# A transformer layer on eight cores: the down projection's two passes cut at 256 instead of 512 tokens, the second over all eight PSUM banks

## The chip, the cores and the metric

One Trainium2 chip, all 8 cores, one program on each with its own slice of the work and no exchange between cores. The time is device microseconds of the slowest core.

## The reference

Layer norm, then attention with ALiBi bias, then a feed-forward branch with Walsh-Hadamard transforms, whose gate multiplies the attention's output (batch 2, 4096 tokens, E = 2048, 16 heads, inner width I = 8192):

```python
xn = layernorm(x)
s = attention(xn)                                  # causal, ALiBi, 16 heads
h = fwht(xn * SU_ug) / 64
u = silu(h @ W_gate.T * sc_gate) * (h @ W_up.T * sc_up)
z = fwht(u * SU_dp) / 64                           # over I = 8192
f = z @ W_down.T * (Wscale_dp * 64)
out = x + s * silu(f)
```

## The kernel before

Each core takes one batch's keys and values and a quarter of its queries: TOKF = 1024 tokens. Everything is held transposed, features on partitions and tokens on columns. A small scheduler (`Sched`) keeps one list of operations per engine. An engine runs its list strictly in the order in which `OP` was called for it, and an operation begins with waits on semaphores (L108 and L125 are the helper's waits). Nothing is reordered.

The program runs in phases: K and V projections (L491, L530), Q (L621), attention (L730 to L773), the output projection (L816), whose result s goes to `s_dram`; then the feed-forward branch. There the up and gate projections (L912) fill `U`, a tile of 64 row blocks (I / 128) of 1024 tokens in SBUF. The transform over I is done in two parts: within 128 rows by a matmul with a Hadamard matrix (L952, evicted by ACT at L958), and over the 64 row blocks by VectorE, in 32 slices of 32 tokens. A slice reads U (L976, L977), makes four rounds in `C1`/`C2` (L996, L998), and its last round writes U back (L1005, L1008).

The down projection, the part in question, follows in two passes over tokens, pass 0 with tokens 0 to 511 and pass 1 with the rest (`FHT` = 512). Each pass has four groups `eog` of 512 output features, that is four blocks `e4` of 128, each of which accumulates in a PSUM bank of its own (`pb`, eight banks of 512 fp32 columns). A group is 16 steps. For each step POOL loads four row blocks x 512 features of `wdT` (L1036, fp32 in memory, bf16 in SBUF, 512 KB there) into one of five ring slots `wdring`, and PE makes 16 matmuls 128x128 by 128x512 (L1048). A load waits for the matmuls of five steps before. Groups alternate between banks 0 to 3 and 4 to 7, so a group's first matmul waits for the evictions of the group before the last. It waits for the transform too: pass 0 for slice 16 (`ev_zH`), pass 1 for slice 32 (`ev_z`).

A finished bank goes through four steps. ACT evicts it with SiLU into `g_st` (L1070), and issues the loads of s (`ss_st`, L1077) and x (`xf_st`, L1083) from its own queue. VectorE combines them (`tensor_mul` into `o_st`, L1089; `tensor_add` into `res_st`, L1093). SP stores the result (L1103). All of these buffers have two halves (`par`), so an eviction waits for the combine of two before (`prev2`). A combine also waits for the store of the one before (`prev_out`):

```python
prev2 = ev_comb.get(gc - 2)
prev_out = ev_outs[gc - 1] if gc >= 2 else None
```

Since the combines are put on VectorE's list after the loop over slices, none can run before slice 32 is done.

Of the kernel before, what the change touches and what calls it, by code (L numbers as in the profile page):

```python
# [9 lines left out]
AF = mybir.ActivationFunctionType  # L10
# [122 lines left out]
def build_program(cfg):  # L133
    S, E, I, QG = cfg.S, cfg.E, cfg.I, cfg.QG
    FT, IT, H = cfg.FT, cfg.IT, cfg.H
    NSLOT, CS = cfg.NSLOT, cfg.CS
    TOKF = cfg.TOKF
# [3 lines left out]
    FH = TOKF // 2  # L141
# [7 lines left out]
    NSL = TOKF // CS  # L149
# [9 lines left out]
    xfT_d = din("xfT", [E, TOKF])  # L159
# [18 lines left out]
    out_d = nc.dram_tensor("out", [E, TOKF], F32, kind="ExternalOutput").ap()  # L178
# [115 lines left out]
    def Uap(it, c0, w):  # L294
        t = Us[it // ITQ]
        base = (it % ITQ) * TOKF
        return t[:, base + c0: base + c0 + w]
# [663 lines left out]
    ev_h2_last = ev_h2_ev[(IT - 1, UPC - 1)]  # L961

    ev_z = None
    ev_zH = None
    for sl in range(NSL):
        sl0 = sl * CS
        ename = "vector"
        cA, cB = C1, C2

        def p4_sA(eng, sl0=sl0, cA=cA):  # L970
            q = ITQ
            for half, (ua, ub) in enumerate(((Us[0], Us[2]), (Us[1], Us[3]))):
                a = ua.rearrange("p (t c) -> p t c", c=TOKF)[:, :, sl0:sl0 + CS]
                b = ub.rearrange("p (t c) -> p t c", c=TOKF)[:, :, sl0:sl0 + CS]
                c3 = cA.rearrange("p (t c) -> p t c", c=CS)
                eng.tensor_add(c3[:, half * q:(half + 1) * q, :], a, b)  # L976
                ins = eng.tensor_sub(  # L977
                    c3[:, 2 * q + half * q:2 * q + (half + 1) * q, :], a, b)
            return ins
        ev_sA = OP(ename, p4_sA,  # L980
                   waits=[ev_h2_last if sl == 0 else ev_z,
                          ev_ug_mm[(IT - 1, 1)] if sl == 0 else None])

        ev_stg = ev_sA
        src, dst = cA, cB
        for st in range(nst2 - 2, -1, -1):
            d = 1 << st
            last = (st == 0)

            def p4_s2(eng, src=src, dst=dst, d=d, last=last, sl0=sl0):  # L990
                if not last:
                    s4 = src.rearrange("p (g two w) -> p g two w", two=2,
                                       w=d * CS)
                    d4 = dst.rearrange("p (g two w) -> p g two w", two=2,
                                       w=d * CS)
                    eng.tensor_add(d4[:, :, 0, :], s4[:, :, 0, :],  # L996
                                   s4[:, :, 1, :])
                    return eng.tensor_sub(d4[:, :, 1, :], s4[:, :, 0, :],  # L998
                                          s4[:, :, 1, :])
                s4 = src.rearrange("p (g two w) -> p g two w", two=2, w=CS)  # L1000
                for uq in range(4):
                    utv = Us[uq].rearrange("p (t two c) -> p t two c", two=2,
                                           c=TOKF)[:, :, :, sl0:sl0 + CS]
                    gg = uq * (ITQ // 2)
                    eng.tensor_add(utv[:, :, 0, :],  # L1005
                                   s4[:, gg:gg + ITQ // 2, 0, :],
                                   s4[:, gg:gg + ITQ // 2, 1, :])
                    ins = eng.tensor_sub(utv[:, :, 1, :],  # L1008
                                         s4[:, gg:gg + ITQ // 2, 0, :],
                                         s4[:, gg:gg + ITQ // 2, 1, :])  # L1010
                return ins
            ev_stg = OP(ename, p4_s2, waits=[ev_stg])
            src, dst = dst, src
        ev_z = ev_stg
        if sl == NSL // 2 - 1:
            ev_zH = ev_z

    ev_wd_ld = {}
    ev_dn_mm = {}
    ev_gs = {}  # L1020
    ev_comb = {}
    ev_outs = []
    gld = 0
    gc = 0
    NEOG = FT // 4
    FHT = FH
    for ps in range(2):
        tk0 = ps * FHT
        ev_zg = ev_zH if ps == 0 else ev_z
        for eog in range(NEOG):  # L1030
            g2 = ps * NEOG + eog
            for it4 in range(IT // K2):
                slot = gld % NWDR
                prev_mm = ev_dn_mm.get(gld - NWDR)
                ev_wd_ld[(ps, eog, it4)] = OP("gpsimd",
                    (lambda eng, eog=eog, it4=it4, slot=slot: eng.dma_start(  # L1036
                        wdring[slot].rearrange("p (b c) -> p b c", b=K2),
                        wdT_d[it4 * K2 * 128:(it4 + 1) * K2 * 128,
                              eog * 512:eog * 512 + 512].rearrange(
                                  "(b p) c -> p b c", p=128))),  # L1040
                    waits=[ev_u_all, prev_mm], dma="wd%d" % slot)

                def p4_dn(eng, eog=eog, it4=it4, slot=slot, tk0=tk0, g2=g2):
                    bk0 = (g2 % 2) * 4
                    for iti in range(K2):
                        it = it4 * K2 + iti
                        for e4 in range(4):
                            ins = eng.matmul(  # L1048
                                pb[bk0 + e4][:, 0:FHT],
                                wdring[slot][:, iti * 512 + e4 * 128:  # L1050
                                             iti * 512 + e4 * 128 + 128],
                                Uap(it, tk0, FHT),
                                start=(it == 0), stop=(it == IT - 1))
                    return ins
                ws = [ev_wd_ld[(ps, eog, it4)]]
                if it4 == 0:
                    ws += [ev_zg]
                    ws += [ev_gs.get((g2 - 2, kkk)) for kkk in range(4)]
                ev_dn_mm[gld] = OP("tensor", p4_dn, waits=ws)
                gld += 1  # L1060

            for e4 in range(4):
                eo = eog * 4 + e4
                par = gc % 2
                bk = (g2 % 2) * 4 + e4
                prev2 = ev_comb.get(gc - 2)
                prev_out = ev_outs[gc - 1] if gc >= 2 else None

                ev_g = OP("scalar", (lambda eng, bk=bk, eo=eo, par=par:
                    eng.activation(g_st[:, par * FHT:(par + 1) * FHT],  # L1070
                                   pb[bk][:, 0:FHT], AF.Silu,
                                   scale=dnvec[:, eo:eo + 1])),
                    waits=[ev_dn_mm[gld - 1], prev2])
                ev_gs[(g2, e4)] = ev_g

                ev_ss = OP("scalar", (lambda eng, eo=eo, tk0=tk0, par=par:
                    eng.dma_start(ss_st[:, par * FHT:(par + 1) * FHT],  # L1077
                                  s_dram[eo * 128:(eo + 1) * 128,
                                         tk0:tk0 + FHT])),
                    waits=ev_sd_all + [prev2, ev_zg], dma="st%d" % par)  # L1080

                ev_xf = OP("scalar", (lambda eng, eo=eo, tk0=tk0, par=par:
                    eng.dma_start(xf_st[:, par * FHT:(par + 1) * FHT],  # L1083
                                  xfT_d[eo * 128:(eo + 1) * 128,
                                        tk0:tk0 + FHT])),
                    waits=[prev2, ev_zg], dma="st%d" % par)

                def p4_comb(eng, par=par):
                    sch.chain("vector", eng, eng.tensor_mul(  # L1089
                        o_st[:, par * FHT:(par + 1) * FHT],  # L1090
                        g_st[:, par * FHT:(par + 1) * FHT],
                        ss_st[:, par * FHT:(par + 1) * FHT]))
                    return eng.tensor_add(  # L1093
                        res_st[:, par * FHT:(par + 1) * FHT],
                        o_st[:, par * FHT:(par + 1) * FHT],
                        xf_st[:, par * FHT:(par + 1) * FHT])
                ev_cb = OP("vector", p4_comb,
                           waits=[ev_g, ev_ss, ev_xf, prev_out])
                ev_comb[gc] = ev_cb

                ev_outs.append(OP("sync", (lambda eng, eo=eo, tk0=tk0,
                                           par=par:
                    eng.dma_start(out_d[eo * 128:(eo + 1) * 128,  # L1103
                                        tk0:tk0 + FHT],
                                  res_st[:, par * FHT:(par + 1) * FHT])),
                    waits=[ev_cb], dma="outd"))
                gc += 1

    n_out = sch.cnt["outd"]
    sch.ops["sync"].append(  # L1110
# [87 lines left out]
```

How the kernel before makes its waits and increments, by code:

```python
    def chain(self, eng_name, E, ins):  # L103
        s = self.sem(self.esem[eng_name] + "ch")
        self.cnt[self.esem[eng_name] + "ch"] += 1
        v = self.cnt[self.esem[eng_name] + "ch"]
        ins.then_inc(self.sems[self.esem[eng_name] + "ch"], 1)
        E.wait_ge(self.sems[self.esem[eng_name] + "ch"], v)
# [7 lines left out]
            def body(E, lst=lst):  # L116
                done = {}
                for fn, ws, ev in lst:
                    need = {}
                    for (s, v, _b) in ws:
                        if v > need.get(s, 0):
                            need[s] = v
                    for s, v in need.items():
                        if v > done.get(s, 0):
                            E.wait_ge(self.sems[s], v)
                            done[s] = v
                    ins = fn(E)
                    if ev is not None:
                        ins.then_inc(self.sems[ev[0]], ev[2])
# [268 lines left out]
        def p1_stats(eng, par=par, ev_s=ev_sq[slab]):  # L398
            for ft in range(FT):
                eng.matmul(pb[0][0:1, 0:128], ones128_b[:],
                           xTb[par][:, ft * 128:ft * 128 + 128],
                           start=(ft == 0), stop=(ft == FT - 1))
            eng.wait_ge(sch.sems[ev_s[0]], ev_s[1])
            for ft in range(FT):
                ins = eng.matmul(pb[0][0:1, 128:256], ones128_b[:],
                                 sq_scr[:, ft * 128:ft * 128 + 128],
                                 start=(ft == 0), stop=(ft == FT - 1))
            return ins
```

## Time and profile before

| | us |
|---|---|
| median of 2 runs | 4943.36 (4925.18 to 4961.55) |
| profiled execution | 4600.18 |
| its span, core 7 | 4598.6 |
| spans of the eight cores | 4572.6 to 4598.6 |
| PE busy in the span | 3423.3 (74%) |
| DVE busy | 1863.6 (41%) |
| ACT busy | 956.5 (21%) |

The profile is that of one execution, which took less than the timed ones; its span is the time from the first to the last instruction of the slowest core. Times within it are microseconds from the span's start. The granted clock is the share of TensorE's full 2.4 GHz.

### The profile page before, as it was taken

To read this page: it belongs to the slowest core of one execution; us is meant where nothing else is said; L and a number is where in the kernel's file an instruction comes from. 1 tells how busy PE (TensorE), PEld (TensorE's weight loads), DVE (VectorE), ACT (ScalarE), POOL (GpSimd) and SP (SyncE) were. 2 spreads that over 40 slices of the span, in tenths; PEclk is the share of its full clock that TensorE was granted. 3 is DMA by queue.
4 is the path that set the end of the run, shared out by engine and by line. 5 is a ranking of instruction groups with operands and counts; after the bars stand their busy time and mean duration, and the time that the engine had idled before them with its cause. 6 is when DMAs were issued, how large, how long until landed. Compare 5 with 4: busy or idle time off the path is not lost.

```text
span 4598.6 us, 61740 instructions; the slowest of 8 cores (4572.6 to 4598.6 us)
## 1 busy us (share of the span) xinstructions
PE 3423.3 (74%) x22715; PEld 1784.6 (39%) x22715; DVE 1863.6 (41%) x3576; ACT 956.5 (21%) x2347; POOL 293.5 (6%) x309
## 2 busy tenths in 40 slices
PE   0499796997995677788884929999999910634887
PEld 0276575765762222222221804444444300211333
DVE  0244444444440166667773060000000079995001
ACT  0121121211211234444442211111111420000000
POOL 0000000000000000000000001111111100100111
PEclk9899898998997777778776959999999965867999
DMA  9323232232324221111104118888889600645999
GB/s 147 28 44 52 42 53 42 43 55 39 51 42 74 61 56 37 46 28 37 37 19 74 40 12 78 76 76 77 75 73 77 66 0 0 89 65 89 177 172 155
DMA packets 633739, 287.94 MB, mean 63 GB/s; under 512 B 520675, under 2 KB 614883, under 8 KB 631267
## 3 DMA queue, kind: packets, MB, share of 16 engines
q0 software_dynamic: 422880, 191.55, 37.5%
q1 hardware_dynamic: 107652, 42.10, 4.2%
q10 hardware_dynamic: 102912, 50.35, 4.2%
q8 instruction: 187, 3.06, 0.3%
q14 instruction: 108, 0.88, 0.1%
HBM read 429.34 MB, written 46.14 MB: 103 GB/s over the span
## 4 chain that ended last, share of the span: by engine, by line
PE 64%; DVE 20%; DMA 6%; issue 3%; SPq 3%; another core or an unknown queue 2%; ACT 1%; DVEq 0%; ACTq 0%; POOLq 0%
PE pb L912 18%; PE pb L530 9%; PE pb L491 9%; PE pb L751 5%; PE pb L734 5%; PE pb L1048 4%; PE pb L730 4%; DMA wdring<-wdT 4%; DVE C L996 3%; DVE C L998 3%; SPq L307 3%; PE pb L816 2%; PE pb L621 2%; DVE rinv L667 2%
## 5 line engine op out<-in xcount | busy, mean ns | idle before, releaser
L912 PE MATMUL pb<-xnTf,wring 128*128 128x512 bf16 x4096 | 889.2, 380 | 5.2 <-DMA wring<-wupT 3.9
L1048 PE MATMUL pb<-U,wdring 128*128 128x512 bf16 x2048 | 457.4, 385 | 419.8 <-DVE U L1008 247.3
L763 DVE SCALAR_TENSOR_TENSOR pb<-mwin_s,slopes_l,pb 128x256 f32<-128x256 f16 x1019 | 484.0, 482 | 471.4 <-PE pb L751 451.4
L912 PEld LDWEIGHTS pb<-xnTf,wring 128*128 128x128 bf16 x4096 | 401.4, 98 | 492.9 <-issue 14.0
L773 ACT ACTIVATE ET<-pb 128x256 bf16<-128x256 f32 x1019 | 390.0, 384 | 486.2 <-DVE pb L763 393.8
L491 PE MATMUL pb<-xnT,wk_b 128*128 128x128 bf16 x8192 | 485.2, 222 | 0.0
L491 PEld LDWEIGHTS pb<-xnT,wk_b 128*128 128x128 bf16 x8192 | 471.5, 99 | 10.9 <-issue 1.0
L530 PE MATMUL pb<-wv_b,xnT 128*128 128x512 bf16 x2048 | 454.8, 383 | 16.9 <-DVE vstg L543 16.9
L1048 PEld LDWEIGHTS pb<-U,wdring 128*128 128x128 bf16 x2048 | 200.1, 99 | 676.9 <-issue 449.4
L936 DVE TENSOR_TENSOR U<-A_st,B_st 128x1024 bf16<-128x1024 f32 x64 | 78.4, 1225 | 830.0 <-ACT B_st L928 830.0
L730 PE MATMUL pb<-ET,vh 128*128 128x256 bf16 x1019 | 331.7, 326 | 9.5 <-DMA vh<-v_scr 4.0
L751 PE MATMUL pb<-q_sb,kh 128*128 128x256 bf16 x1019 | 307.1, 323 | 25.2 <-DMA kh<-k_scr 25.2
L734 PE MATMUL pb<-ET,ones_b 128*1 128x256 bf16 x1019 | 311.3, 305 | 0.0
L530 PEld LDWEIGHTS pb<-wv_b,xnT 128*128 128x128 bf16 x2048 | 200.5, 99 | 257.1 <-issue 28.1
L506 ACT ACTIVATE kstg<-pb,bk_l 128x128 bf16<-128x128 f32 x512 | 188.0, 367 | 243.4 <-PE pb L491 243.1
L543 DVE TENSOR_TENSOR vstg<-pb,bvB 128x512 bf16<-128x512 f32 x128 | 88.1, 691 | 352.0 <-PE pb L530 313.1
L466 DVE TENSOR_TENSOR xn_scr<-xTb,rstdB 128x128 f32<-128x128 bf16 x640 | 186.8, 292 | 76.3 <-ACT mrstdB L459 8.3
L1070 ACT ACTIVATE g_st<-pb,dnvec 128x512 bf16<-128x512 f32 x32 | 22.0, 687 | 863.7 <-PE pb L1048 546.7
L734 PEld LDWEIGHTS pb<-ET,ones_b 128*1 128x1 bf16 x1019 | 80.5, 79 | 268.3 <-issue 247.6
L674 PE MATMUL pb<-rinv,ones_f 1*128 1x256 f32 x128 | 63.3, 587 | 161.9 <-DVE rinv L667 161.9
L471 DVE TENSOR_TENSOR xnT<-xn_scr,mrstdB 128x128 bf16<-128x128 f32 x512 | 149.5, 292 | 54.1 <-DVE xn_scr L466 1.5
L751 PEld LDWEIGHTS pb<-q_sb,kh 128*128 128x128 bf16 x1019 | 95.9, 99 | 192.8 <-issue 129.9
(85 smaller groups left out, 2446.1 us busy)
## 6 DMA issues: line engine op xcount, KB each, us to landing
wdring<-wdT POOLq DMA_DIRECT2D x128, 512.0 KB, 12.6
wring<-wupT POOLq DMA_DIRECT2D x64, 512.0 KB, 9.5
wring<-wgT POOLq DMA_DIRECT2D x64, 512.0 KB, 9.0
xTb<-xT POOLq DMA_DIRECT2D x32, 512.0 KB, 8.7
k_scr<-kstg ACTq DMA_DIRECT2D x32, 512.0 KB, 5.0
v_scr<-vstg ACTq DMA_DIRECT2D x128, 128.0 KB, 1.9
kh<-k_scr SPq DMA_DIRECT2D x16, 1024.0 KB, 5.4
vh<-v_scr SPq DMA_DIRECT2D x16, 1024.0 KB, 9.5
```

The lines of the kernel that those rows point to most:

```text
L466: sch.chain("vector", eng, eng.tensor_mul(xn_scr[:], xTb[par][:, ft * 128:ft * 128 + 128], rstdB[:, par * 128:par * 128 + 128]))
L471: ins = eng.tensor_sub(dst, xn_scr[:], mrstdB[:, par * 128:par * 128 + 128])
L491: ins = eng.matmul(bank[:, 0:128], wk_b[:, (ft * H + hch) * 128:(ft * H + hch) * 128 + 128], xnT2[par2][:, ft * 128:ft * 128 + 128], start ...
L506: return eng.activation(kstg[par][:, hch * 128:hch * 128 + 128], bank[:, 0:128], AF.Identity, bias=bk_l[:, hch:hch + 1])
L530: ins = eng.matmul(bank[:, 0:512], xnT2[par2][:, ft * 128:ft * 128 + 128], wv_b[:, ft * E + vch * 512:ft * E + vch * 512 + 512], start=(ft ...
L730: eng.matmul(pvb[:, 0:QG], vh[hp][:, rho * 128:rho * 128 + 128], ETs[e4][:], start=(idx == 0), stop=(idx == W - 1))
L734: return eng.matmul(pb[6 + par][0:1, 0:QG], ones128_b[:], ETs[e4][:], start=(idx == 0), stop=(idx == W - 1))
L751: return eng.matmul(pb[b4][:, 0:QG], kh[hp][:, rho * 128:rho * 128 + 128], q_ap, start=True, stop=True)
L763: eng.scalar_tensor_tensor(pb[b4][:, 0:QG], mwin_s[:, coff:coff + QG], slopes_l[:, h:h + 1], pb[b4][:, 0:QG], ALU.mult, ALU.add)),
L773: eng.activation(ETs[e4][:], pb[b4][:, 0:QG], AF.Exp)),
L912: ins = eng.matmul(pb[bk0 + u][:, 0:UCH], wring[slot][:, ft * 128:ft * 128 + 128], xnTf[:, ft * TOKF + u * UCH:ft * TOKF + u * UCH + UCH], ...
L1048: ins = eng.matmul(pb[bk0 + e4][:, 0:FHT], wdring[slot][:, iti * 512 + e4 * 128: iti * 512 + e4 * 128 + 128], Uap(it, tk0, FHT), start=(it ...
```

## The change

The passes are no longer equal. Pass 0 takes tokens 0 to 255 in one chunk; pass 1 takes tokens 256 to 1023 in two chunks of 384. The gate of a pass is now worked out from its last token: slice 8 for pass 0, slice 32 for pass 1. In pass 0 a group still uses four banks, in turn. In pass 1 a group has two chunks x four feature blocks and uses all eight banks, so each step makes 32 matmuls of 384 columns from one load of the ring. The number of ring loads stays 128 (2 passes x 4 groups x 16), the columns multiplied stay the same, the matmuls grow from 2048 to 3072 (1024 of 256 columns and 2048 of 384), and evictions, combines and stores from 32 to 48 (16 of 256 columns, 32 of 384). The waits for banks are kept by bank (`bank_owner`) instead of by group.

```diff
-        if sl == NSL // 2 - 1:
-            ev_zH = ev_z
+        ev_z_at[sl] = ev_z
...
-    FHT = FH
-    for ps in range(2):
-        tk0 = ps * FHT
-        ev_zg = ev_zH if ps == 0 else ev_z
+    q4 = TOKF // 4
+    passes = [(0, [q4]), (q4, [3 * TOKF // 8, 3 * TOKF // 8])]
+    for ps, (tk0, chunks) in enumerate(passes):
+        gate_sl = (tk0 + sum(chunks) + CS - 1) // CS - 1
+        ev_zg = ev_z_at[gate_sl]
+        nck = len(chunks)
         for eog in range(NEOG):
             g2 = ps * NEOG + eog
+            if nck == 1:
+                bks = [(g2 % 2) * 4 + e4 for e4 in range(4)]
+            else:
+                bks = list(range(8))
...
                     for iti in range(K2):
                         it = it4 * K2 + iti
-                        for e4 in range(4):
-                            ins = eng.matmul(
-                                pb[bk0 + e4][:, 0:FHT],
...
-                                Uap(it, tk0, FHT),
-                                start=(it == 0), stop=(it == IT - 1))
+                        off = 0
+                        for ci, cw in enumerate(chunks):
+                            for e4 in range(4):
+                                ins = eng.matmul(
+                                    pb[bks[ci * 4 + e4] if len(chunks) > 1
+                                       else bks[e4]][:, 0:cw],
...
+                                    Uap(it, tk0 + off, cw),
+                                    start=(it == 0), stop=(it == IT - 1))
+                            off += cw
...
                 if it4 == 0:
                     ws += [ev_zg]
-                    ws += [ev_gs.get((g2 - 2, kkk)) for kkk in range(4)]
+                    ws += [bank_owner.get(b) for b in bks]
...
-            for e4 in range(4):
-                eo = eog * 4 + e4
-                par = gc % 2
-                bk = (g2 % 2) * 4 + e4
+            off = 0
+            for ci, cw in enumerate(chunks):
+                for e4 in range(4):
+                    eo = eog * 4 + e4
+                    bk = bks[ci * 4 + e4] if nck > 1 else bks[e4]
+                    par = gc % 2
+                    c0 = tk0 + off
...
+                    bank_owner[bk] = ev_g
```

The eviction, the two loads, the combine and the store are the same but for their width `cw` and their place `c0`.

PE's queue where the last group of pass 0 goes over to the first of pass 1, before:

```order
5189 L1048 MATMUL pb<-U_96,wdring_119 128x512 [waits s_wd3]
5190 L1048 MATMUL pb<-U_96,wdring_119 128x512 x15
5191 L1048 MATMUL pb<-U_93,wdring_120 128x512 [waits s_wd4,s_dve,s_act]
5192 L1048 MATMUL pb<-U_93,wdring_120 128x512 x15
5193 L1048 MATMUL pb<-U_93,wdring_116 128x512 [waits s_wd0]
```

The same place of the changed kernel (`U_93` to `U_96` are the four parts of U, `wdring_116` to `_120` the five slots; `s_act` stands for the banks):

```order
5189 L1056 MATMUL pb<-U_96,wdring_119 128x256 [waits s_wd3]
5190 L1056 MATMUL pb<-U_96,wdring_119 128x256 x15
5191 L1056 MATMUL pb<-U_93,wdring_120 128x384 [waits s_wd4,s_dve,s_act]
5192 L1056 MATMUL pb<-U_93,wdring_120 128x384 x31
5193 L1056 MATMUL pb<-U_93,wdring_116 128x384 [waits s_wd0]
```

One load of a slot now serves 32 matmuls of pass 1, and the wait on `s_act` is for the last of eight evictions instead of the last of four of the group before the last.

ACT's queue at the beginning of the down projection, before:

```order
1935 L1070 ACTIVATE g_st<-pb,dnvec 128x512 [waits s_pe]
1936 L1077 DMA ss_st<-s_scr 128x512 [waits s_dve]
1937 L1083 DMA xf_st<-xfT 128x512
1938 L1070 ACTIVATE g_st<-pb,dnvec 128x512
1939 L1077 DMA ss_st<-s_scr 128x512
1940 L1083 DMA xf_st<-xfT 128x512
1941 L1070 ACTIVATE g_st<-pb,dnvec 128x512 [waits s_dve]
```

And in the changed kernel:

```order
1935 L1084 ACTIVATE g_st<-pb,dnvec 128x256 [waits s_pe]
1936 L1093 DMA ss_st<-s_scr 128x256 [waits s_dve]
1937 L1100 DMA xf_st<-xfT 128x256
1938 L1084 ACTIVATE g_st<-pb,dnvec 128x256
1939 L1093 DMA ss_st<-s_scr 128x256
1940 L1100 DMA xf_st<-xfT 128x256
1941 L1084 ACTIVATE g_st<-pb,dnvec 128x256 [waits s_dve]
```

Only the widths moved: the third eviction waits for VectorE's first combine in both.

## Rows read from the trace of the kernel before

**Rows 1.** The cores' spans, slowest and fastest, with mean granted clock
```profile
core 4: 4572.6 us, clock 0.870
...
core 7: 4598.6 us, clock 0.866
```
**Rows 2.** The page's 40 slices of the span, in tenths busy, PE and DVE
```profile
PE   0499796997995677788884929999999910634887
...
DVE  0244444444440166667773060000000079995001
```
**Rows 3.** Timeline of PE from 3700 on: start, duration, count, idle before and releaser
```profile
3949.30 112.34 PE L1048 MATMUL pb<-U,wdring 128*128 128x512 bf16 x512 [247.29 <-DVE U L1008]
4198.54 29.43 PE L1048 MATMUL pb<-U,wdring 128*128 128x512 bf16 x128 [136.90 <-ACT g_st L1070]
4228.69 7.07 PE L1048 MATMUL pb<-U,wdring 128*128 128x512 bf16 x32 [0.72 <-DMA wdring<-wdT]
...
4491.07 34.69 PE L1048 MATMUL pb<-U,wdring 128*128 128x512 bf16 x160 [0.23 <-DMA wdring<-wdT]
...
4546.31 32.93 PE L1048 MATMUL pb<-U,wdring 128*128 128x512 bf16 x144 [2.34 <-DMA wdring<-wdT]
```
**Rows 4.** Timeline of DVE where the last slice ends
```profile
4194.40 0.42 DVE L1008 TENSOR_TENSOR U<-C 128x256 bf16<-128x256 f32 x1
4194.74 0.68 DVE L1089 TENSOR_TENSOR o_st<-g_st,ss_st 128x512 f32<-128x512 bf16 x1
```
**Rows 5.** Windows of core 7: busy time of PE, PEld, DVE, ACT, POOL; clock; DMA share; GB/s
```profile
3949.00:4062.00 113.00, 112.34 (x512) 50.45 (x512) 108.32 (x148) 1.38 (x2) 22.97 (x31) 0.98 1.04 144
4062.00:4198.00 136.00, 0.00 (x0) 0.00 (x0) 129.75 (x178) 0.98 (x2) 0.74 (x1) 0.51 0.07 12
4198.00:4390.00 192.00, 175.40 (x785) 76.28 (x786) 19.38 (x28) 10.02 (x15) 35.55 (x48) 0.98 1.10 175
4390.00:4580.00 190.00, 169.69 (x753) 73.39 (x751) 16.62 (x24) 7.48 (x11) 31.85 (x43) 0.97 1.05 166
4580.00:4599.00 19.00, 0.00 (x0) 0.00 (x0) 5.54 (x8) 2.15 (x4) 0.00 (x0) 0.61 0.43 138
```
**Rows 6.** Groups of the page: busy us, mean ns of one, idle before
```profile
L912 PE MATMUL pb<-xnTf,wring 128*128 128x512 bf16 x4096 | 889.2, 380 | 5.2 <-DMA wring<-wupT 3.9
L1048 PE MATMUL pb<-U,wdring 128*128 128x512 bf16 x2048 | 457.4, 385 | 419.8 <-DVE U L1008 247.3
```
**Rows 7.** Waits from 3700 on: us in total, times, longest
```profile
PE pb L1048 <- DMA wdring<-wdT: 35.5, 28, 4.0
```
**Rows 8.** Short matmuls in a free stream, and their weight loads by group
```profile
268.82 12.78 PE L491 MATMUL pb<-xnT,wk_b 128*128 128x128 bf16 x224
...
L491 PEld LDWEIGHTS pb<-xnT,wk_b 128*128 128x128 bf16 x8192 | 471.5, 99 | 10.9 <-issue 1.0
```
**Rows 9.** DMA issues: count, KB each, median us to landing
```profile
wq_b<-wqT POOLq DMA_DIRECT2D x1, 8192.0 KB, 53.1
```
**Rows 10.** Timeline of DVE and ACT after the last matmul
```profile
4579.39 0.69 ACT L1070 ACTIVATE g_st<-pb,dnvec 128x512 bf16<-128x512 f32 x1 [42.01 <-PE pb L1048]
...
4582.70 0.69 DVE L1089 TENSOR_TENSOR o_st<-g_st,ss_st 128x512 f32<-128x512 bf16 x1 [29.38 <-DMA xf_st<-xfT]
...
4586.86 0.69 DVE L1089 TENSOR_TENSOR o_st<-g_st,ss_st 128x512 f32<-128x512 bf16 x1 [2.67 <-DMA out<-res_st]
...
4594.70 0.69 DVE L1089 TENSOR_TENSOR o_st<-g_st,ss_st 128x512 f32<-128x512 bf16 x1 [2.20 <-DMA out<-res_st]
```
**Rows 11.** The same after the group that ends at 4323.7: eviction, then the combines
```profile
4323.81 0.69 ACT L1070 ACTIVATE g_st<-pb,dnvec 128x512 bf16<-128x512 f32 x1 [42.74 <-PE pb L1048]
...
4333.17 0.69 DVE L1089 TENSOR_TENSOR o_st<-g_st,ss_st 128x512 f32<-128x512 bf16 x1 [34.72 <-DMA xf_st<-xfT]
...
4343.12 0.69 DVE L1089 TENSOR_TENSOR o_st<-g_st,ss_st 128x512 f32<-128x512 bf16 x1 [8.46 <-DMA out<-res_st]
...
4352.58 0.69 DVE L1089 TENSOR_TENSOR o_st<-g_st,ss_st 128x512 f32<-128x512 bf16 x1 [7.98 <-DMA out<-res_st]
...
4360.80 0.69 DVE L1089 TENSOR_TENSOR o_st<-g_st,ss_st 128x512 f32<-128x512 bf16 x1 [6.73 <-DMA out<-res_st]
```
**Rows 12.** The chain of waits at the end: start, us, what
```profile
4579.26 0.02 issue
...
4584.26 2.50 DMA out<-res_st
...
4588.42 2.50 DMA out<-res_st
```

More of the change, by code:

```diff
@@ L963, in build_program @@
     ev_z = None
-    ev_zH = None
+    ev_z_at = {}
     for sl in range(NSL):
@@ L1022, in build_program @@
     ev_outs = []
+    bank_owner = {}
     gld = 0
@@ L1041, in build_program, with p4_dn @@
                     waits=[ev_u_all, prev_mm], dma="wd%d" % slot)
-                def p4_dn(eng, eog=eog, it4=it4, slot=slot, tk0=tk0, g2=g2):
-                    bk0 = (g2 % 2) * 4
+                def p4_dn(eng, eog=eog, it4=it4, slot=slot, tk0=tk0,
+                          chunks=chunks, bks=bks):
                     for iti in range(K2):
                         it = it4 * K2 + iti
-                        for e4 in range(4):
-                            ins = eng.matmul(
-                                pb[bk0 + e4][:, 0:FHT],
-                                wdring[slot][:, iti * 512 + e4 * 128:
-                                             iti * 512 + e4 * 128 + 128],
-                                Uap(it, tk0, FHT),
-                                start=(it == 0), stop=(it == IT - 1))
+                        off = 0
[4 more added lines that the diff above has]
+                                       else bks[e4]][:, 0:cw],
+                                    wdring[slot][:, iti * 512 + e4 * 128:
+                                                 iti * 512 + e4 * 128 + 128],
+                                    Uap(it, tk0 + off, cw),
+                                    start=(it == 0), stop=(it == IT - 1))
+                            off += cw
                     return ins
@@ L1057, in build_program @@
                     ws += [ev_zg]
-                    ws += [ev_gs.get((g2 - 2, kkk)) for kkk in range(4)]
+                    ws += [bank_owner.get(b) for b in bks]
                 ev_dn_mm[gld] = OP("tensor", p4_dn, waits=ws)
                 gld += 1
-            for e4 in range(4):
-                eo = eog * 4 + e4
-                par = gc % 2
-                bk = (g2 % 2) * 4 + e4
[L1066 to L1107, printed above, removed]
@@ new lines, in build_program, with p4_comb @@
+            off = 0
[5 more added lines that the diff above has]
+                    c0 = tk0 + off
+                    prev2 = ev_comb.get(gc - 2)
+                    prev_out = ev_outs[gc - 1] if gc >= 2 else None
+                    ev_g = OP("scalar", (lambda eng, bk=bk, eo=eo, par=par,
+                                         cw=cw:
+                        eng.activation(g_st[:, par * FH:par * FH + cw],
+                                       pb[bk][:, 0:cw], AF.Silu,
+                                       scale=dnvec[:, eo:eo + 1])),
+                        waits=[ev_dn_mm[gld - 1], prev2])
+                    ev_gs[(g2, ci * 4 + e4)] = ev_g
+                    bank_owner[bk] = ev_g
+                    ev_ss = OP("scalar", (lambda eng, eo=eo, c0=c0, par=par,
+                                          cw=cw:
+                        eng.dma_start(ss_st[:, par * FH:par * FH + cw],
+                                      s_dram[eo * 128:(eo + 1) * 128,
+                                             c0:c0 + cw])),
+                        waits=ev_sd_all + [prev2, ev_zg], dma="st%d" % par)
+                    ev_xf = OP("scalar", (lambda eng, eo=eo, c0=c0, par=par,
+                                          cw=cw:
+                        eng.dma_start(xf_st[:, par * FH:par * FH + cw],
+                                      xfT_d[eo * 128:(eo + 1) * 128,
+                                            c0:c0 + cw])),
+                        waits=[prev2, ev_zg], dma="st%d" % par)
+                    def p4_comb(eng, par=par, cw=cw):
+                        sch.chain("vector", eng, eng.tensor_mul(
+                            o_st[:, par * FH:par * FH + cw],
+                            g_st[:, par * FH:par * FH + cw],
+                            ss_st[:, par * FH:par * FH + cw]))
+                        return eng.tensor_add(
+                            res_st[:, par * FH:par * FH + cw],
+                            o_st[:, par * FH:par * FH + cw],
+                            xf_st[:, par * FH:par * FH + cw])
+                    ev_cb = OP("vector", p4_comb,
+                               waits=[ev_g, ev_ss, ev_xf, prev_out])
+                    ev_comb[gc] = ev_cb
+                    ev_outs.append(OP("sync", (lambda eng, eo=eo, c0=c0,
+                                               par=par, cw=cw:
+                        eng.dma_start(out_d[eo * 128:(eo + 1) * 128,
+                                            c0:c0 + cw],
+                                      res_st[:, par * FH:par * FH + cw])),
+                        waits=[ev_cb], dma="outd"))
+                    gc += 1
+                off += cw
```

## The prediction, made before the changed kernel ran

> **What bounds the kernel now.** I read from the outside in: the cores, the page's slices, and then only the end of the program, since nothing ahead of the last phase is changed. The eight cores end within 0.6% of each other [rows 1], so one core stands for all. The time line of the slices [rows 2] shows two PE holes near the end, where DVE works alone: that is the transform over 64 row blocks (32 slices of 32 tokens), of which the down projection is the reader.
>
> The PE timeline [rows 3] gives the program's last 900 us. PE is idle for 247.29 us until the 16th slice is done, then runs 512 matmuls of 512 columns in 112.34 us without one wait on data, is idle again for 136.90 us, and from 4198.54 runs the other 1536 until 4546.31 + 32.93 = 4579.24. The second hole is the important one. Its releaser is the eviction g_st on ACT, and the DVE rows [rows 4] say why that eviction was late: the combines (L1089, L1093) stand behind all 32 slices in DVE's queue. The slices' last piece is at 4194.40, and the first combine starts at 4194.74. Since the third eviction waits for the first combine, no third group of banks could be had before. So of pass 0's four groups only two ran under the transform: 512 of 2048 matmuls, a quarter of the columns. The last slice's end, about 4195, does not depend on PE, so it stays where it is. All that the change is worth is then decided in the stretch after it: 4198.5 to 4598.6 = 400.1 us.
>
> What limits that stretch? PE is busy in 89 to 91% of it [rows 5] with matmuls that cost 457.4/2048 = 0.223 us by their group and 34.69/160 = 0.217 when they run freely [rows 3, 6]. PE waits 35.5 us in 28 pieces for the weight ring [rows 7]. The DMA share stands at 1.05 to 1.10 in it [rows 5]. 1536 matmuls are 96 loads of the ring in 380.7 us, 3.97 us each, against 16 x 0.217 = 3.47 of matmul. So weights and PE are nearly balanced, and weights win slightly while combines share the DMA engines.
>
> **The change part by part.**
>
> Pass widths. Pass 0 is cut from 512 tokens to 256 with an earlier gate (slice 8 of 32), pass 1 grows to 768. But the queue order on DVE is the same, so again only groups 0 and 1 of pass 0 can run before the slices end. They need 32 loads; at 3.97 us each that is 127 us. A slice takes (4194.7 - 3949.3)/16 = 15.3 us [rows 3, 4], so the new gate, eight slices ahead of the old one, opens at about 3826, and the two groups are done by 3955, long before 4195. Cost: nothing, and the cover has 240 us to spare; and the earlier gate earns nothing, since this hole was never short. What was hidden before was 512 x 512 columns; now it is 512 x 256. Half of the hidden work comes out into the open: 131,072 columns, about 55 us of PE at 0.217 per 512 if PE sets the pace.
>
> Rest of pass 0 (groups 2 and 3, 512 matmuls of 256 columns). Between the 128-column row (12.78/224 = 0.057 us) and the 512-column one (0.217) a straight line gives 0.110 for 256 columns and 0.164 for 384 [rows 3, 8]. Even the 128-column ones stream faster than their weight loads' 98 ns rows, so short matmuls have no floor that matters here. PE would need 512 x 0.110 = 57 us, 1.8 per ring load. The weights can't follow: five loads lie ready, 27 must come. Bounds for a load: 53.1/16 = 3.32 us, the large wq_b load cut into pieces of 512 KB [rows 9], and 3.97 with full combines beside it. Combines of half size run here, so I take 3.7: 27 x 3.7 = 100, with the first and last loads' matmuls 104. (57 if the ring could be fed at PE's pace; 111 at the high end.) In this part the change makes the starved side worse.
>
> From pass 0 to pass 1. The first matmul of each pass-1 group now waits for all eight banks, where it used to wait for four banks given up one group earlier. Behind that wait stand the group's 512 matmuls, and behind those ACT's evictions and POOL's ring loads, which find no free slot. To free the last bank of pass 0, ACT must evict number 15, which waits for combine 13. At the program's end [rows 10] PE's last matmul ends at 4579.26, the first combine starts at 4582.70, and the next ones follow about 4.15 us apart, since each waits for the output DMA of the one before (2.50 us in the chain [rows 12]). That is with idle DMAs. With the ring filling, the first came 9.4 us after its eviction and the periods were 9.95, 9.46 and 8.22 [rows 11]. Idle: 3.4 + 3.8 + 1.8 = 9; loaded: 9.4 + 9.2 + 1.8 = 20. I take 15.
>
> Pass 1. 4 x 512 matmuls of 384 columns: 2048 x 0.164 = 335 us. Each ring load now serves 32 matmuls = 5.2 us, above 3.97, so the 35.5 us of waits for weights go; PE sets the pace. That is the gain, and it is small.
>
> Three drains between groups of pass 1. PE stops at the last matmul, and the eighth eviction waits for the sixth combine: 3.4 to the first, 5 periods, a combine of 1.2, an eviction of 0.6. A period at 384 columns: 4.15 less a quarter each of two 0.69 us VectorE pieces, with the output DMA left at 2.50, is 3.8. So 24 us, and 2 more for ring loads still in flight: 26 each, 78 in all. Bounds: 21 if the DMA shrinks with its bytes, 57 if the loaded periods of [rows 11] hold. I choose near the idle end because PE takes 5.2 us over a load, so one or two are in flight when it stops, not five. Before, these drains lay under the other four banks' matmuls.
> [...]
>
> Restarts. After the idle 136.90 us the first 128 matmuls took 29.43 instead of 27.8 [rows 3]; in the idle hole the granted clock is 0.51, the lower level of 1.2 GHz, and 0.97 to 0.98, nearly always 2.4 GHz, where PE works [rows 5]. Five starts x 1.6 = 8 us.
>
> Tail. Eight combines follow the last matmul instead of four: 3.4 + 7 x 3.8 + 3.5 = 33 us, where it was 19.3.
>
> Sum after 4198.5: 104 + 15 + 335 + 78 + 8 + 33 = 573 us, against 400.1: 173 more. The profiled execution took 4600.18 us (its span of 4598.6 and 1.6 around it), so it would become 4773, a ratio of 1.0376. The runs shown have a median of 4943.36, 7.5% above the profiled one, which the trace does not explain. I carry the ratio: 5129 (adding 173 gives 5116).
>
> **The rivals.**
>
> A, drains under load: the ring and the combines' own loads keep DMA full, and each drain costs 57, the first boundary 20. For it speak the 9.2 us periods in all of the stretch while the ring works; against it that the ring is full and silent some 15 us after PE stops. 573 + 93 + 5 = 671: 4871, ratio 1.059, 5235.
>
> B, weights arrive faster than I think: rest of pass 0 at PE's pace (57) and a boundary of 9. For it speaks that with the DMA share at 1.04 PE did not wait once for weights [rows 5, 3], so 3.5 us is no proven floor; against it the 28 waits after 4198. 573 - 47 - 6 = 520: 4720, ratio 1.026, 5072.
>
> C, not slower: all of pass 0 runs under the transform. With half the width, its 64 loads need 254 us, and from 3826 there are 370. Then 104 + 15 + 2 fall away: 452, 52 us more than now, 4652, ratio 1.011, 4999. It decides at combine 0: only if combines get onto DVE before the last slice. Against it stand DVE's rows [rows 4] and an order of the queue that the change leaves alone. Even then the drains must vanish too for a gain.
>
> D, shorter matmuls in a free stream. If the 0.217 us are a pace set by weights rather than by the array, halving the ring's traffic in pass 1 speeds matmuls up: at an assumed 0.114 us for 384 columns pass 1 takes 233, 471 in all, 4671, ratio 1.015, 5020. The gate's projections at 0.217 (889.2/4096 [rows 6]), with 5.2 us of idle in all, speak against it. The source of that 0.114 is the Trainium skill (TensorE: Matmul & The Clock Gate, "Back-to-back issue gap"), which gives about 131 ns for 512 columns and 81 for 128 in a stream of load and matmul pairs, and a line between them gives 114; this trace has 217 and 57 and disagrees at both ends.
>
> **How the numbers follow.** Forecast 0.75, A 0.10, B 0.10, C 0.03, D 0.01, and 0.01 for what I don't see. The forecast's own bounds: low 94 + 9 + 335 + 63 + 8 + 30 = 539 (5092), high 111 + 20 + 337 + 120 + 8 + 35 = 631 (5191). Reaching to B, and for the step from profile to median, the range is 5060 to 5200; A, C and D fall out, 0.14. Within 2% (about what a measurement of this kernel can tell from no change) lie C and D: 0.04. No case gives over 2% faster: 0.01 for the unseen. Slower by over 2%: 0.95.
>
> **What would show it.** PE idle from 3955 or so to 4195 though pass 0 began near 3826; 512 matmuls of 256 columns in about 104 us after it with many waits on wdring; three waits of PE on g_st of 24 to 30 us, at equal distances of about 110 us, with six combines in each; no wait on wdring in pass 1; eight outputs after the last matmul. I am wrong if a third group of pass 0 starts before 4190, if PE's waits at the boundaries of pass 1 are under 15 or over 40 us, or if a 384-column matmul costs other than 0.16 to 0.17 us.

## The result and the profile after

The changed kernel is slower: the ratio to the kernel before is 1.0384, 95% interval 1.0362 to 1.0405. The forecast had a ratio of 1.0376, but named 5129 us with a range of 5060 to 5200; the median of 11 runs is 4986.68 and falls outside it.

These two fit together only so: in some executions of either kernel the four cores of one die, or of both, show a lower granted clock (a mean down to 0.77 instead of 0.85 to 0.86 in the changed kernel), the two runs behind the 4943.36 of before are as slow as those, and without them before takes 4589 to 4615 us and the changed kernel 4771 to 4778 (4800.6 in its profiled execution), which are the times that are compared from here on.

Core 7 of the changed kernel can be laid beside core 7 of before. Cores of the changed kernel:

```profile
core 0: 4799.0 us, clock 0.853
...
core 7: 4771.0 us, clock 0.859
```

4771.0 - 4598.6 = 172.4 us more; the sum had 173. From PE's third group to the end it is 4771.0 - 4194.6 = 576.4 us instead of 400.1, that is 176.3 more; core 7 came to that group 3.9 us earlier than in the profile of before. (Core 0 is later still because its last slice ends 20 us later than that of core 7, at 4212.7, through phases that the change doesn't touch.)

The PE timeline of core 7, in the columns of [rows 3]:

```profile
3823.60 10.52 PE L1056 MATMUL pb<-U,wdring 128*128 128x256 bf16 x80 [124.29 <-DVE U L1008]
3834.32 1.91 PE L1056 MATMUL pb<-U,wdring 128*128 128x256 bf16 x16 [0.21 <-DMA wdring<-wdT]
...
4194.62 12.77 PE L1056 MATMUL pb<-U,wdring 128*128 128x256 bf16 x96 [269.30 <-ACT g_st L1084]
4211.15 1.91 PE L1056 MATMUL pb<-U,wdring 128*128 128x256 bf16 x16 [3.76 <-DMA wdring<-wdT]
...
4303.76 2.41 PE L1056 MATMUL pb<-U,wdring 128*128 128x256 bf16 x16 [0.29 <-DMA wdring<-wdT]
4321.41 85.26 PE L1056 MATMUL pb<-U,wdring 128*128 128x384 bf16 x512 [15.23 <-ACT g_st L1084]
4431.54 84.82 PE L1056 MATMUL pb<-U,wdring 128*128 128x384 bf16 x512 [24.87 <-ACT g_st L1084]
4542.20 85.79 PE L1056 MATMUL pb<-U,wdring 128*128 128x384 bf16 x512 [25.85 <-ACT g_st L1084]
4652.60 85.22 PE L1056 MATMUL pb<-U,wdring 128*128 128x384 bf16 x512 [24.60 <-ACT g_st L1084]
```

The whole story stands in these lines. Pass 0 starts 126 us earlier than before and then stands still for 269.30 us: the hole has grown, not gone. What starts at 4194.62 runs freely for six steps (96 matmuls) and then goes in steps of 16 matmuls, most of them 1.9 us long and with a wait for weights behind them, until 4306.2. Then come four blocks of 512 matmuls without one wait on the ring, each behind a wait for an eviction.

The DVE timeline where the last slice ends answers to [rows 4]:

```profile
4191.69 0.42 DVE L1008 TENSOR_TENSOR U<-C 128x256 bf16<-128x256 f32 x1
4192.02 0.41 DVE L1106 TENSOR_TENSOR o_st<-g_st,ss_st 128x256 f32<-128x256 bf16 x1
```

The first combine still comes straight behind the last slice, and PE's third group 2.6 us after it.

Waits of core 7 from 3700 on, as in [rows 7]:

```profile
PE pb L1056 <- ACT g_st L1084: 359.9, 5, 269.3
...
PE pb L1056 <- DMA wdring<-wdT: 83.0, 51, 4.3
```

Five waits for evictions instead of one. The waits for weights have more than doubled from 35.5 us, and all are in pass 0; but of the 83.0 us only 43.3 come after the last slice, where they cost time. The rest lie in the first two groups, ahead of the long hole. The group of PE's instructions from 4190 on shows it:

```profile
L1056 PE MATMUL pb<-U,wdring 128*128 128x256 bf16 x512 | 68.2, 295 | 312.6 <-ACT g_st L1084 269.3 <-DMA wdring<-wdT 43.3
```

Windows of the same core, columns as in [rows 5]:

```profile
4194.00:4306.00 112.00, 68.07 (x512) 52.15 (x512) 8.50 (x20) 4.27 (x9) 22.96 (x31) 0.92 1.09 166
4321.00:4407.00 86.00, 85.26 (x512) 50.63 (x512) 1.70 (x4) 0.44 (x2) 11.11 (x15) 0.97 0.64 99
4407.00:4431.00 24.00, 0.00 (x0) 0.00 (x0) 6.70 (x12) 4.08 (x8) 0.74 (x1) 0.58 0.57 149
4738.00:4771.00 33.00, 0.00 (x0) 0.00 (x0) 8.93 (x16) 4.62 (x8) 0.00 (x0) 0.56 0.40 119
```

In the rest of pass 0 the DMA share is 1.09 with PE busy 61% of the time; in a block of pass 1 it is 0.64 with PE full. In the first drain (third row) no engine is busy over a third of the time. The tail takes 33 us (last row).

### The profile page after: what moved, and what is told of

It reads as the page before. It is cut to its first block, busy times and chain, and to the rows that moved or that the text cites. A ratio compares the mean times of both kernels' runs of the same rounds, so it can differ in the third digit from the quotient of the medians.

```text
span 4799.0 us, 63980 instructions; the slowest of 8 cores (4762.5 to 4799.0 us)
## 1 busy us (share of the span) xinstructions
PE 3459.1 (72%) x23739; PEld 1898.8 (40%) x23739; DVE 1868.7 (39%) x3608; ACT 960.0 (20%) x2363; POOL 293.5 (6%) x309
## 4 chain that ended last, share of the span: by engine, by line
PE 66%; DVE 19%; DMA 5%; issue 3%; SPq 3%; another core or an unknown queue 2%; ACT 1%; DVEq 0%; ACTq 0%; POOLq 0%
PE pb L912 18%; PE pb L530 9%; PE pb L491 9%; PE pb L1056 8%; PE pb L751 5%; PE pb L734 5%; PE pb L730 4%; DVE C L996 3%; DVE C L998 3%; SPq L307 3%; PE pb L816 2%; PE pb L621 2%; DVE rinv L667 2%; DMA wdring<-wdT 2%
## 5 line engine op out<-in xcount | busy, mean ns | idle before, releaser
L1056 PE MATMUL pb<-U,wdring 128*128 128x384 bf16 (+1 forms) x3072 | 476.7, 318 | 570.4 <-ACT g_st L1084 367.8
L1056 PEld LDWEIGHTS pb<-U,wdring 128*128 128x128 bf16 x3072 | 305.9, 101 | 741.1 <-issue 593.9
L530 PE MATMUL pb<-wv_b,xnT 128*128 128x512 bf16 x2048 | 473.4, 394 | 18.8 <-DVE vstg L543 18.8
L1084 ACT ACTIVATE g_st<-pb,dnvec 128x384 bf16<-128x384 f32 (+1 forms) x48 | 26.2, 546 | 1043.3 <-PE pb L1056 581.7
L1106 DVE TENSOR_TENSOR o_st<-g_st,ss_st 128x384 f32<-128x384 bf16 (+1 forms) x48 | 24.7, 514 | 529.7 <-DMA xf_st<-xfT 387.7
```

What stands on the lines that cost most here:

```text
L530: ins = eng.matmul(bank[:, 0:512], xnT2[par2][:, ft * 128:ft * 128 + 128], wv_b[:, ft * E + vch * 512:ft * E + vch * 512 + 512], start=(ft ...
L1056: ins = eng.matmul(pb[bks[ci * 4 + e4] if len(chunks) > 1 else bks[e4]][:, 0:cw], wdring[slot][:, iti * 512 + e4 * 128: iti * 512 + e4 * 1 ...
```

## The experiments

All are the changed kernel (4771 to 4778 us) or the kernel before with one edit or a few. They ran in three sets, each on a chip of its own with the kernel before beside it, which took 4582 to 4585 us in the set of x_gate16, x_noload, x_inter and x_store2, 4582 to 4586 in that of x_3pass, x_inter_store2, b_inter and b_inter_store2, and 4589 to 4597 in that of x_first, b_inter_again and b_best. So some 10 us between two sets need not come from the kernels; in the first set x_gate16 stands for the changed kernel.

**x_gate16: is the early gate worth anything?**

```diff
-        gate_sl = (tk0 + sum(chunks) + CS - 1) // CS - 1
+        gate_sl = NSL // 2 - 1 if ps == 0 else NSL - 1
```

> The changed kernel with one edit: pass 0 (256 tokens) waits for slice 16 again instead of slice 8. My theory: the early gate earns nothing, since the third group's banks wait for the first combine, behind slice 32. Time within 5 us of the changed kernel's 4771 to 4778 us; PE begins the down projection near 3950 instead of 3830 and the matmuls after the transform start at the same distance from the last slice. Rival (the early start is worth its 120 us): about 4890.

4767.4 and 4768.3 us, ratio 1.0403 (1.0373 to 1.0433), which is the changed kernel's 1.0384 within both intervals. Its PE timeline, core 3:

```profile
3937.08 10.20 PE L1056 MATMUL pb<-U,wdring 128*128 128x256 bf16 x80 [247.31 <-DVE U L1008]
...
4185.12 10.75 PE L1056 MATMUL pb<-U,wdring 128*128 128x256 bf16 x80 [146.26 <-ACT g_st L1084]
```

Pass 0 begins over 110 us later, and the only thing that changes is which of the two idle times is the longer one. The early gate is worth nothing in this kernel.

**x_noload: do weights set the pace of the rest of pass 0?**

```diff
+                if ps == 0 and eog >= 2:
+                    ev_wd_ld[(ps, eog, it4)] = last_ld[slot]
+                else:
+                  last_ld[slot] = ev_wd_ld[(ps, eog, it4)] = OP("gpsimd",
...
```

> The changed kernel without the 32 ring loads of groups 2 and 3 of pass 0; their matmuls read what earlier loads left in the slots, so part of the output is computed from other weights. My theory: in the changed kernel this part takes 111 us because weights arrive every 3.5 us or so; with none to wait for it takes PE's own 57 us plus a start, 57 to 62, and with the DMAs idle the combines come every 4 us, so that pass 1 starts after a wait of 9 instead of 16. In all 55 to 62 us less, about 4714. Rival (PE or evictions set the pace there): under 15 us less.

4715.4 us (expected: 4714). PE timeline, core 6:

```profile
4190.00 58.09 PE L1060 MATMUL pb<-U,wdring 128*128 128x256 bf16 x512 [273.45 <-ACT g_st L1088]
4264.38 85.76 PE L1060 MATMUL pb<-U,wdring 128*128 128x384 bf16 x512 [16.30 <-ACT g_st L1088]
```

58.09 us for the 512 matmuls instead of 111.6: the weights held them back, by 53 us. A 256-column matmul costs 0.113 us. (That the DMA engines set the pace of the weights, and not the five slots of the ring, is likely from the DMA share of 1.09 above; no run changed the number of slots.) One part of the expectation failed: the wait ahead of pass 1 stayed at 16.30 and did not go to 9. I had thought the DMAs idle there. They are not: POOL's timeline shows the loads held up so far leave all at once as the last slots come free, beside ACT's loads of s and x.

```profile
4241.66 0.74 POOL L1046 DMA_DIRECT2D wdring<-wdT  x1 [336.69 <-PE pb L1060]
...
4248.63 0.74 POOL L1046 DMA_DIRECT2D wdring<-wdT  x1 [1.01 <-PE pb L1060]
```

So 53 us of the expected 55 to 62 are found in these steps. The total agrees: on the same chip x_gate16 took 4767.4 us, 52 more than the 4715.4 here. That 4714 was expected and 4715.4 came is in part luck, since it was reckoned from the 4771 of another chip.

**x_inter: is it VectorE's queue order that holds pass 0 back?** The loop over slices is made a function, `slices_to(n)`, that puts the slices up to n on VectorE's list if they aren't there yet.

```diff
+                    slices_to(12 + gc)
                     ev_cb = OP("vector", p4_comb,
                                waits=[ev_g, ev_ss, ev_xf, prev_out])
```

> The changed kernel with the sixteen combines of pass 0 put between the slices of the transform on VectorE, one after each of slices 13 to 28, instead of behind slice 32. My theory (the queue order on VectorE holds pass 0 back): all four groups of pass 0 run under the transform, and pass 1 starts right behind slice 32. The transform gets 16 x 0.9 = 14 us longer; the 111 us and the 16 us of wait go: 110 to 115 us less than the changed kernel, about 4662, ratio to before about 1.012 (1.009 to 1.015). Rival (banks or weights hold pass 0 back): groups 2 and 3 still after slice 32, no less than 4750.

4655.1, 4657.5 and 4662.2 us (4662 expected), ratio 1.0165 (1.0135 to 1.0194); the ratio expected, 1.009 to 1.015, was reckoned from a slower before. Against x_gate16 on the same chip it is 105 to 113 us less. PE timeline, core 2:

```profile
4201.43 84.75 PE L1064 MATMUL pb<-U,wdring 128*128 128x384 bf16 x512 [164.63 <-DVE U L1010]
4313.07 85.23 PE L1064 MATMUL pb<-U,wdring 128*128 128x384 bf16 x512 [26.90 <-ACT g_st L1092]
```

Behind the last slice there is only pass 1. So the prediction's rival C has the right price (4652, though it had no term for the combines' 14 us on VectorE), and it needs this edit to come about: what held pass 0 back is the place of the combines in VectorE's queue. The banks that PE waited for were only kept by it, and weights come in time for four groups. The three drains of 27 us are still there, and they, the longer tail and the combines' time in the transform are what keeps this kernel slower than before: about 81, 13 and 14 us, less 40 that PE saves on the last 768 tokens' matmuls and waits for weights (341 against 380.7).

**x_store2: what is a drain made of?**

```diff
-                    prev_out = ev_outs[gc - 1] if gc >= 2 else None
+                    prev_out = ev_outs[gc - 2] if gc >= 2 else None
...
-                        waits=[ev_cb], dma="outd"))
+                        waits=[ev_cb], dma="outd%d" % par))
```

> The changed kernel with the stores on two semaphores, one for each half of res_st, and a combine waiting for the store of two before instead of the one before. My theory: a drain is a chain of combine and store, 3.6 us a link; without the store in it the chain is eviction, loads of s and x, combine, about 5 us for two links. Each of the three drains goes from 26 to 29 us down to about 16 to 18, the tail from 32 to about 25, the wait ahead of pass 1 from 16 to about 14: 35 to 45 us less in all, ratio to before about 1.030. Rival (the drains are set by the loads of s and x or by the DMA engines): drains still over 24 us and under 10 us less in all.

4740.5 and 4774.3 us, ratio 1.038 with a wide interval (1.0293 to 1.0468), which alone decides nothing. In the run of 4740.5 all eight cores end at 4720.3 to 4738.9 us, where those of x_gate16's profiled execution end at 4749.4 to 4766.7: some 28 us less, not the 35 to 45 expected. The profiled execution is the one of 4774.3; there cores 0 to 3 (granted clock 0.860 and 0.861) end at 4729.0 to 4734.4, and cores 4 to 7 (0.849 to 0.856) at 4760.8 to 4772.7. PE timeline of core 1:

```profile
4308.39 85.14 PE L1056 MATMUL pb<-U,wdring 128*128 128x384 bf16 x512 [12.12 <-ACT g_st L1084]
4413.06 85.70 PE L1056 MATMUL pb<-U,wdring 128*128 128x384 bf16 x512 [19.54 <-ACT g_st L1084]
4519.79 85.25 PE L1056 MATMUL pb<-U,wdring 128*128 128x384 bf16 x512 [21.03 <-ACT g_st L1084]
4624.87 85.61 PE L1056 MATMUL pb<-U,wdring 128*128 128x384 bf16 x512 [19.83 <-ACT g_st L1084]
```

Drains of 20 instead of 25 to 29: over all cores the 24 drains are 19.2 to 21.6 us here, 24.2 to 27.5 in x_gate16. So the chain of stores set them. They don't reach the 16 to 18 that I expected; the chain of waits in the drain before 4519.79 shows the first loads at fault.

```profile
4500.37 7.30 DMA xf_st<-xfT
...
4509.53 3.71 DMA xf_st<-xfT
...
4515.11 2.48 DMA xf_st<-xfT
```

The load of x takes 7.30 us while the last ring loads land (issued at 4494.10 and 4499.30, 6.3 to 8.2 us each), and 2.48 when the ring is full.

**x_first: can that first load be had earlier?** The loads of s and x are put ahead of the eviction in ACT's queue.

> The changed kernel with the loads of s and x ahead of the eviction in ACT's queue, so that those of the first two banks of a group are issued while the group's matmuls run. My theory: a drain starts with eviction and loads (3.3 to 7 us to the first combine, then a chain of stores at 3.6); with the loads long done the first combine follows its eviction, under 1 us after PE's last matmul. 3 to 6 us less in each of the three drains, in the wait ahead of pass 1 and in the tail: 15 to 22 us less, ratio to before about 1.034. Rival (the stores alone set the drains): under 5 us less.

4768 to 4779 us, ratio 1.0394 (1.0376 to 1.0412): no gain. A miss, and the rival was right. DVE timeline of core 7 in the second drain, where PE stops at 4505.2:

```profile
4506.14 0.56 DVE L1106 TENSOR_TENSOR o_st<-g_st,ss_st 128x384 f32<-128x384 bf16 x1 [79.58 <-ACT g_st L1098]
...
4512.69 0.56 DVE L1106 TENSOR_TENSOR o_st<-g_st,ss_st 128x384 f32<-128x384 bf16 x1 [5.33 <-DMA out<-res_st]
...
4516.29 0.56 DVE L1106 TENSOR_TENSOR o_st<-g_st,ss_st 128x384 f32<-128x384 bf16 x1 [2.38 <-DMA out<-res_st]
```

The first combine does come 0.9 us after PE's last matmul, 3 us earlier than in the changed kernel. But now the first store meets the loads of the ring, and takes 5.16 us in the chain of waits, where in the changed kernel's first two drains it took 3.13 and 3.48; and each later eviction, the last one too, starts behind the issue of two loads, 1.0 us after its combine instead of 0.1. PE's three waits are 25.27, 25.33 and 25.56 us, against 24.87, 25.85 and 24.60. All cores show the same: from PE's stop to the first combine 0.9 us instead of 3.2 to 5.2, from the first to the second combine 7.1 on average instead of 5.4, and a drain of 26.8 instead of 26.5.

```profile
4507.43 5.16 DMA out<-res_st
```

Ahead of pass 1 and in the tail some 4 and 2 us are gained, too little to be seen in the time.

**x_3pass: drains or weights?**

```diff
-    passes = [(0, [q4]), (q4, [3 * TOKF // 8, 3 * TOKF // 8])]
+    w3 = 3 * TOKF // 8
+    passes = [(0, [q4]), (q4, [w3]), (q4 + w3, [w3])]
```

> The changed kernel with its pass 1 cut in two passes of 384 tokens, each with four banks in turn: 192 ring loads instead of 128, no group with eight banks. My theory: no drains (26 to 29 us three times goes) and a shorter tail (18 instead of 32), but PE needs 16 x 0.166 = 2.7 us for a step and weights come every 3.8 us: 111 for the rest of pass 0, then 128 loads x 3.8 = 486 instead of 341 + 83 + 16, tail 18. About 4815, ratio to before 1.050 (1.04 to 1.06). Rival (the eight-bank group is the main loss, DMA is not short): 16 x 128 x 0.166 = 341 us for the two passes, in all about 4670.

The lower of its two times is 4784.9 us, about 1.044 times before on the same chip, which is in the expected 1.04 to 1.06. The direction holds; the time was 30 us too high, since both the rest of pass 0 (105 us instead of 111) and the steps of the other passes were faster. In the profiled execution core 4 shows in the groups of PE's instructions:

```profile
L1057 PE MATMUL pb<-U,wdring 128*128 128x384 bf16 x2048 | 366.2, 335 | 100.0 <-DMA wdring<-wdT 97.5 <-ACT g_st L1085 1.9
```

366.2 + 97.5 = 464 us for 128 steps, 3.62 us each, where I had 3.8. So four banks in turn cost some 20 us more for the last 768 tokens than eight banks with drains, and the rival (4670, drains the main loss) is out: with eight banks, 341 of matmul, 75 of drains, 15 of wait and a tail of 33 is 464; with four banks, 466 and a tail of 19 is 485.

**b_inter, b_inter_again, b_inter_store2, b_best: the kernel before with the cause removed.** The same `slices_to`, on the two equal passes of before.

```diff
+                slices_to(20 + gc)
                 ev_cb = OP("vector", p4_comb,
                            waits=[ev_g, ev_ss, ev_xf, prev_out])
```

> The kernel before (two passes of 512 tokens) with the combines of pass 0 put between the slices, one after each of slices 21 to 32, the rest behind them. My theory: all of pass 0's 64 ring loads fit under the second half of the transform (from 3949, at 3.5 to 3.97 us each, to about 4190), the transform ends some 12 x 1.4 = 17 us later, about 4212, and only pass 1 is left: 64 loads at 3.97 = 254 us less the five that lie ready, then the tail of 19 us. About 4485, ratio to before 0.975 (0.970 to 0.980). Rival (DMA traffic of combines and loads slows the slices or pass 0, so that it runs over): 4520 or more.

> The kernel before with interleaved combines alone, once more. My theory: as the first time, 4468 to 4485; ratio to before 0.975 (0.970 to 0.980).

> The same, and the stores on two semaphores by half. My theory: with banks taken in turns no drain is exposed, so only the tail of four combines gets shorter: 3 to 5 us less than with the interleaved combines alone, about 4481.

> The kernel before with interleaved combines, stores on two semaphores and loads ahead of the eviction. My theory: only the tail is exposed, so 3 us less than the 4460 to 4468 of the version without the last edit, which cannot be told from it: ratio to before 0.972 to 0.974.

With the combines alone the runs to compare are 4467.9 in b_inter, and 4472.2 and 4473.9 in b_inter_again: about 0.974 of before on the same chip, without an interval. With the stores on two semaphores as well: 0.9735 (0.9707 to 0.9763), lowest 4460.1. With the loads first too: 0.9723 (0.9704 to 0.9742), lowest 4463.5. The three can't be told from each other; all are faster than both kernels. The ratio of b_inter is as expected; the 4485 us expected of it and the 4481 of b_inter_store2 were 11 to 21 us too high. PE timeline of b_inter_store2, core 7:

```profile
3946.21 101.96 PE L1055 MATMUL pb<-U,wdring 128*128 128x512 bf16 x464 [247.31 <-DVE U L1010]
...
4184.52 5.30 PE L1055 MATMUL pb<-U,wdring 128*128 128x512 bf16 x16 [2.55 <-DMA wdring<-wdT]
4204.91 67.78 PE L1055 MATMUL pb<-U,wdring 128*128 128x512 bf16 x304 [15.09 <-DVE U L1010]
```

All of pass 0 lies under the transform and ends 15 us ahead of it. Its windows, pass 0 and pass 1:

```profile
3946.00:4190.00 244.00, 228.66 (x1024) 100.17 (x1024) 234.53 (x324) 8.28 (x13) 46.66 (x63) 0.98 1.09 165
4205.00:4451.00 246.00, 226.91 (x1024) 99.73 (x1023) 23.02 (x34) 10.31 (x15) 43.69 (x59) 0.98 1.06 168
```

Here PE is busy for 228.66 us and VectorE for 234.53 of the same 244: 94 and 96% of the time. Expected were 254 us for 64 loads; it is 246, 3.84 each.

The last of the kernels was the changed one with both edits:

> The changed kernel with both edits: combines of pass 0 between slices 13 to 28, and stores on two semaphores. My theory: the savings add, since one is ahead of pass 1 and the other in its drains and tail: 4657 less three times 9 and 7, about 4622, ratio to before 1.008.

4627.7 and 4629.6 us (4622 expected), ratio 1.0096 (1.0067 to 1.0125): the savings add, and the wide pass is still no match for two equal ones. Once all of pass 0 is hidden, its width decides what is left in the open: 341 us of matmul for 768 tokens here, 227 for 512 tokens in b_inter_store2. To these 114 us come the three drains of 20 us; b_inter_store2 gives back some 19 in waits for weights.

## Why the prediction was right or wrong

The sum after the last slice, step by step, on core 7 of the changed kernel:

| step | predicted | measured |
|---|---|---|
| rest of pass 0 | 104 | 111.6 (4194.62 to 4306.2) |
| wait ahead of pass 1 | 15 | 15.2 |
| matmuls of pass 1, with restarts | 343 | 341.1 |
| three drains | 78 | 75.3 |
| tail | 33 | 33.2 |
| sum | 573 | 576.4 |
| the same stretch of before | 400.1 | 400.1 |

- **What failed** is the last step, "The runs shown have a median of 4943.36, 7.5% above the profiled one, which the trace does not explain. I carry the ratio: 5129". The profile gave 4773, which the changed kernel's 4771 to 4778 bear out. I took a gap that I could not explain for a property of the kernel, and the range (5060 to 5200) didn't hold the case that it would go away. The runs show no one factor like it: before took 4589.4 to 4614.7 us in six of its ten runs and 4803.9 to 4961.6 in the other four, the changed kernel 4770.9 to 4778.2 in five of eleven and 4986.7 to 5204.2 in six. The median 4986.68 is the lowest of those six, so 4773 would have missed it as well. What makes one execution of a kernel so much longer than another stays open.
- **The sum came out near in part by luck.** 173 was forecast and 176.3 measured for the stretch: the rest of pass 0 took 7.6 us more, matmuls and drains together 4.6 less.
- **The rest of pass 0** was short not in its price of a load but at its start. From PE's seventh step (4211.15) to the last (4303.76) a step comes every 3.70 us, the 3.7 of the prediction; but the seventh step comes 16.5 us after the first, where two loads at 3.7 us had been counted, since the first load leaves only when a slot is free (POOL issues it at 4198.74) and needs its time to land. So the whole passed even the upper bound of 111. In the first two groups, with no combines beside them, a step comes every 3.43 us (3837.74 to 3923.41), not 3.97. x_noload shows that weights set the rest of pass 0 (58 us without them), so rival B, PE's pace, is out.
- **The drains** were sized well with the idle end of the rows, but two errors cancel in it. A period on core 7 is 3.6 us (3.8 predicted), since the store went from 2.50 us to 2.2 to 2.5; the prediction's 4.15 also was the two longest of the three links in [rows 10], which are 4.0 on average. Against that the first combine came 3.8 us after the matmuls in the first drain instead of 3.4, and the second 4.5 us after the first. Rival A, 57 us a drain, is out: the 24 drains of the eight cores took 24.1 to 29.4 us, and, as the prediction had it, only one or two ring loads are in flight when PE stops (on core 7 one is issued every 5.2 us, and lands after 5.4 to 7.0).
- **The hidden part.** That nothing could run ahead of the combines is shown by three runs: the gate's place doesn't matter (x_gate16), and moving the combines frees pass 0 in both kernels (x_inter, b_inter). Rival C had the mechanism of the better kernel.
- **Rival D** (matmuls sped up by lighter weight traffic) is out: 341.1/2048 = 0.167 us with restarts, 0.164 predicted. The 81 and 131 ns that the Trainium skill gives for 128 and 512 columns (TensorE: Matmul & The Clock Gate, "Back-to-back issue gap") are not what this case shows: 0.057 us and 0.217 [rows 3, 8].

## What to carry to other kernels

Look at the consumer's place in an in-order queue before moving a gate: two idle holes of PE had different releasers (the slices at one, the combines queued behind all slices at the other), and only the second one mattered. Then give the hidden pass as many tokens as the transform can cover. When a group of matmuls takes all eight banks, price the drain as a chain (eviction, load, combine, store, times the links before the last bank is free), for it is no longer under anything. And make a forecast in microseconds from an execution whose clocks are known, and say which executions it is meant for: here the ratio survived a bad base, the number didn't.

## What the runs showed that I had not expected

- Moving loads earlier doesn't shorten a drain if stores follow: in x_first the contention with the ring moved from the load of x to the first store (5.16 us instead of 3.13). Both are small transfers that meet the last one or two 512 KB loads of the ring.
- The store's time falls more slowly than its size: 2.50 us for 256 KB [rows 12], 2.16 to 2.31 mostly for 192 KB, 1.9 for 128 KB in x_noload with no ring loads beside it (median to landing). Halving the bytes takes off a quarter. By bytes alone 192 KB would take 1.9 and 128 KB 1.25. The Trainium skill (DMA: Bandwidth & Descriptors, "Anatomy of one DMA") gives a fit of about 2.0 us and bytes over 436 GB/s, but for DMAs that GpSimd issues; these stores are issued by SP, and the estimate from it, 2.45 us for 192 KB and 2.30 for 128 KB, is above what they take.
- VectorE and PE ran side by side for 244 us, busy 96% and 94% of it, and PE's matmuls kept their 0.22 us: 228.66/1024 = 0.223 with VectorE at work, 226.91/1024 = 0.222 in pass 1 without it.
